# Moving the experts' weighing and the first batch's key squares from VectorE to ScalarE

## What is computed

```python
# layer 0, feed-forward: 8 experts, 128 wide, two per token
expert_w = jnp.einsum('tk,tke->te', top_k_weights, one_hot)
h1 = jnp.einsum('th,efh->tef', x, W1)
h3 = jnp.einsum('th,efh->tef', x, W3)
g = jax.nn.silu(h1) * h3 * expert_w[:, :, None]
out = jnp.einsum('tef,ehf->th', g, W2)

# layer 1, cross-attention: keys and queries normalised per head
def _rmsnorm(t):
    return t * jax.lax.rsqrt(jnp.mean(t * t, axis=-1, keepdims=True) + EPS)
```

## Time and profile before

| what | value |
|---|---|
| median of 3 runs (lowest to highest) | 1713.43 us (1712.78 to 1719.2) |
| profiled execution | 1715.07 us |
| its span in the trace | 1713.2 us |
| TensorE busy | 1599.9 us, 93% |
| VectorE busy | 1390.3 us, 81% |
| ScalarE busy | 1380.8 us, 81% |
| GpSimd busy | 1149.0 us, 67% |

### The profile page before, as it was taken

How to read it: one execution, slowest core, us unless ns; L and a number is a source line. 1 busy time by engine, 2 the same in 40 slices (tenths; PEclk the granted TensorE clock), 3 DMA queues, 4 the chain that set the end, 5 groups by cost and what they waited for, 6 DMA issues and landing times. The chain is left out here.

```text
span 1713.2 us, 43864 instructions
## 1 busy us (share of the span) xinstructions
PE 1599.9 (93%) x15829; PEld 1012.0 (59%) x16022; DVE 1390.3 (81%) x3487; ACT 1380.8 (81%) x2317; POOL 1149.0 (67%) x1770
## 2 busy tenths in 40 slices
PE   3799999999999899999999999988998999999997
PEld 1466777767767677767777777766563333333332
DVE  8889999999999989999989888889996755555422
ACT  4688888888888788878878888874337999999996
POOL 3558778787787877788888788865775655545200
PEclk9799999999999999999999999998999999999998
DMA  4299999999989999999989999997323232222100
GB/s 175 80 182 199 200 210 199 198 217 214 199 189 200 196 195 184 226 207 205 194 186 219 221 203 200 204 196 183 115 44 113 44 80 39 45 39 45 28 12 14
DMA packets 608872, 261.11 MB, mean 152 GB/s; under 512 B 576528, under 2 KB 581648, under 8 KB 607248
## 3 DMA queue, kind: packets, MB, share of 16 engines
q1 hardware_dynamic: 604432, 258.05, 70.4%
q10 hardware_dynamic: 4224, 0.25, 0.2%
HBM read 99.15 MB, written 17.29 MB: 68 GB/s over the span
## 5 line engine op out<-in xcount | busy, mean ns | idle before, releaser
L1754 PE MATMUL pv<-PT,VV 128*128 128x256 bf16 (+1 forms) x2880 | 341.5, 275 | 13.1 <-DMA PT<-PB 12.9
L1494 ACT ACTIVATE PB<-S,rsum 128x1024 bf16<-128x1024 f32 (+1 forms) x256 | 246.4, 988 | 105.9 <-DVE rsum L1260 81.0
L1754 PEld LDWEIGHTS pv<-PT,VV 128*128 128x128 bf16 (+1 forms) x2880 | 281.0, 99 | 81.6 <-issue 36.3
L1734 PE MATMUL score<-KK,QT 128*128 128x512 bf16 (+2 forms) x1795 | 314.6, 318 | 12.3 <-DVE mxp L1229 5.4
L1251 DVE SCALAR_TENSOR_TENSOR PB<-S,rsum,PB 128x1024 bf16<-128x1024 f32 (+1 forms) x256 | 295.8, 1156 | 2.7 <-ACT PB L1494 2.7
L1734 PEld LDWEIGHTS score<-KK,QT 128*128 128x128 bf16 x1920 | 158.2, 98 | 142.8 <-DVE mxp L1229 11.3
L1484 ACT ACTIVATE S<-S,nmx 128x1601 f32<-128x1601 f32 x128 | 210.2, 1642 | 7.3 <-DVE nmx L1241 7.2
L2621 ACT ACTIVATE P<-score 128x1024 f32<-128x1024 f32 x196 | 199.1, 1060 | 9.5 <-PE score L2713 5.9
L1072 POOL TENSOR_SCALAR S<-S,rsum 128x256 f32<-128x256 f32 x128 | 70.6, 551 | 130.5 <-DVE rsum L1260 116.4
L1613 PE MATMUL tb<-stage,wsb 128*128 128x512 bf16 x767 | 149.3, 337 | 5.8 <-DVE stage L631 3.9
L2733 PE MATMUL pv<-P,V 128*9 128x256 f32 (+1 forms) x2288 | 152.2, 380 | 1.3 <-ACT P L2621 0.8
(11 more groups left out here) (274 smaller groups left out, 3677.2 us busy)
## 6 DMA issues: line engine op xcount, KB each, us to landing
x<-rs_d SPq DMA_DIRECT2D x16, 936.0 KB, 5.1
rsb<-rs_d SPq DMA_DIRECT2D x16, 936.0 KB, 5.4
wsb<-w_split SPq DMA_DIRECT2D x46, 256.0 KB, 4.7
wsb<-w_split SPq DMA_DIRECT2D x23, 512.0 KB, 4.9
wpr<-in_wprojT SPq DMA_DIRECT2D x23, 512.0 KB, 6.6
context_d<-stage SPq DMA_DIRECT2D x16, 400.2 KB, 3.9
l_ctx<-context_d SPq DMA_DIRECT2D x4, 1601.0 KB, 7.4
rawh<-in_w_all SPq DMA_DIRECT2D x12, 512.0 KB, 5.7
```

Of the source, the lines that this page charges most:

```text
L1494: e.activation(m.PB[n % 2][:, 2 * a:a + b], m.S32[n % 2][:, a:b], ACT.Copy, scale=m.rsum[n % 2][:, 1:2]).then_inc(s["p_hi"], 1)
L1734: i = e.matmul(m.score[:, at:at + b - a], qt[:, kind, qp, q * P:(q + 1) * P], kk[:, kp, a:b], start=(k == 0), stop=(k == 2))
L1754: i = e.matmul(m.pv[:, at:at + 256], vv[0:rows, v, t, :], m.PT[k % 2][0:rows, turned(c, a), :], start=(c == first and r == 0), stop=(c == ...
```

## The change

Two pieces of VectorE's work go to ScalarE. The weighing of a half step, one VectorE instruction over 512 columns with a broadcast operand, becomes four ScalarE activations over 128 columns, each with one expert's weight as a per-partition factor (`act_weigh`). It is called behind `act_turn(n - 1)` in the loop, for step 0 behind the preparation of its chunk and for step 1 behind the cast of w2. The square of kn, for the first batch only, becomes an activation behind the value copy; VectorE's sum waits for it on `l1_sq`.

```diff
@@ attention of ScalarE, at it == NGB
             act_up(e, m, s, 0)
             for what, c in ffn_slots(0):
                 act_prepare(e, m, s, 0, what, c)
+            act_weigh(e, m, s, 0)
             act_up(e, m, s, 1)
             act_raw_high(e, m, s, 2)
+            act_weigh(e, m, s, 1)
@@
+def act_weigh(e, m, s, n):
+
+    t, hf, i = n // 2, n % 2, n % 2
+    e.wait_ge(s["f_act"], n + 1)
+    e.wait_ge(s["route_step"], ROUTER_STEPS * (1 if t < EARLY else 2))
+    if n >= 2:
+        e.wait_ge(s["f_turned"], n - 1)
+    for j in range(EH):
+        x = hf * EH + j
+        r = e.activation(m.f_g[i][:, j * FF:(j + 1) * FF], m.f_th[i][:, j * FF:(j + 1) * FF], ACT.Copy,
+                         scale=m.route["ew"][:, t, x:x + 1])
+    r.then_inc(s["f_gate"], 1)
@@ dve_up
     e.tensor_tensor(th[:, :], th[:, :], h3, ALU.mult).then_inc(s["f_act"], 1)
-    e.wait_ge(s["f_act"], n + 1)
-    if n >= 2:
-        e.wait_ge(s["f_turned"], n - 1)
-    w = m.route["ew"][:, t, hf * EH:(hf + 1) * EH].unsqueeze(2).broadcast_to([P, EH, FF])
-    e.tensor_tensor(m.f_g[i][:, :].rearrange("p (a b) -> p a b", a=EH),
-                    th[:, :].rearrange("p (a b) -> p a b", a=EH), w, ALU.mult).then_inc(s["f_gate"], 1)
@@ act_feed_forward
         if n <= 2 * NT:
             act_turn(e, m, s, n - 1)
+        if 2 <= n < 2 * NT:
+            act_weigh(e, m, s, n)
@@ dve_prepare, "product"
-        e.wait_ge(s["l1_kn"], k + 1)
-        e.tensor_tensor(m.l1_sq[0:rows, :], kn[0:rows, :], kn[0:rows, :], ALU.mult).then_inc(s["l1_sq"], 1)
+        if b:
+            e.wait_ge(s["l1_kn"], k + 1)
+            e.tensor_tensor(m.l1_sq[0:rows, :], kn[0:rows, :], kn[0:rows, :], ALU.mult).then_inc(s["l1_sq"], 1)
         e.wait_ge(s["l1_sq"], k + 1)
@@ act_prepare, "product", b == 0
+        k, rows = place(b, c), l1_rows(c)
         product_out(e, m, s, b, c)
+        e.wait_ge(s["l1_kn"], k + 1)
+        e.wait_ge(s["l1_ss"], k)
+        e.activation(m.l1_sq[0:rows, :], m.l1_kn[k % 3][0:rows, :], ACT.Square).then_inc(s["l1_sq"], 1)
```

## The result

The changed kernel took 1721.01 us in the median of 22 runs (1712.88 to 1724.43), the kernel before 1716.87 in the median of 22 (1710.04 to 1722.14). The ratio is 1.0024, with a 95% interval of 1.0012 to 1.0035: some 4.1 us slower, between 2.1 and 6.0. That is less than the 0.5% (8.6 us) up to which the prediction calls a time "same". The forecast was 1717.1 with a range up to 1720.6, so the time lies 0.4 above the range, while the step from before to after (+3.65 forecast) lies inside the measured interval. The base moved instead: the median of three runs was 1713.43, that of 22 runs 1716.87.

A forecast was written before the change was run, and what follows sets the result against it. The prediction took TensorE's 5.63 us step as the bound, VectorE only during the backlog of steps 8 to 11. Start 0.77, stage end 1.58 and clock 1.3 summed to 3.65 on 1713.43: 1717.1, range 1711.8 to 1720.6.

The forecast's parts named there:

- The loop over two engines: Feed-forward steps: VectorE's products, ScalarE's weigh, kn, V, square, then VectorE's sum and stacking form a loop of 5.46 us.
- The working through the steps: Steps 8 to 15, worked out instruction by instruction: the backlog remains and down(15) starts 1.58 us late without the clock.
- The prices on ScalarE: Per step, four weighing activations take 1.30 us, 1.20 until the next start; a square takes 0.40.
- The start: Stage start: square and weighing delay tanh(1) by 1.47 us, 0.45 returned by a faster GpSimd subtraction; everything to down(0) 0.77 late.
- The clock at the end: A 3.2 us TensorE wait ahead of down(14) lowers the granted clock, doubling down(14)'s 12 matmuls: 1.3 us.
- rival 4: Something outside the stage moves by over 0.5% either way; chance 0.05 slower, with the runs' scatter, 0.02 faster.
- Rival 1: Stage follows TensorE's pace alone and the kernel becomes faster, by 0.8 or 1.45 us, to 1712.0; chance 0.22.
- Rival 2: ScalarE's order costs 2.35 us but neither TensorE hole, at stage start or end, lowers the clock: 1715.8; chance 0.2.
- Rival 3: Both holes lower the clock: 5.35 us slower, 1718.8, or near 1720.5 with the upper ScalarE price; chance 0.16.

The follow-up runs named there:

- e1_weigh_only: The changed kernel with the squares back on VectorE, so only the weighing is on ScalarE; ratio to before 1.0017.
- e4_filled: The changed kernel with ten unused TensorE matmuls ahead of down(14); ratio to before 1.0001.
- e5_start: The changed kernel with weigh(0) moved ahead of the first chunk's kn and V on ScalarE; ratio to before 1.0013.
- e2: The changed kernel with the weighing back on VectorE, so only the squares are on ScalarE; ratio to before 0.9979.
- e7: The kernel before with only the two long tanh of steps 8 and 9 moved earlier on ScalarE; ratio to before 1.0011.
- e8: The changed kernel with the weighing back on VectorE and the two long tanh moved earlier on ScalarE; ratio to before 0.9989.
- e11: The kernel before once more, unedited; one run, 1715.72 us.
- e3: The changed kernel with the two long tanh of steps 8 and 9 moved earlier on ScalarE, ahead of the turn's copy; ratio to before 0.9990.
- e10: The changed kernel once more, unedited; ratio to before 1.0019.
- e6: The changed kernel with both the two long tanh earlier and weigh(0) ahead of the first kn; 1712.65 us beside 1715.47, ratio 0.9978.
- e9: e6 with six unused TensorE matmuls in each of three holes, ahead of down(0), down(14) and down(15); ratio to before 0.9989.

## Why the prediction was right or wrong

**The loop over two engines: right.** I had put it at 5.46, and the products stand 5.44 apart, at 1266.80 and 1272.24 and so on to 1288.56. One correction: e1_weigh_only shows that the loop is there without the square on ScalarE, through kn. The square is only one of its links.

**The working through the steps: right.** Against the start of up(8), in us, predicted and measured: down(8) 13.53 and 13.41, chunk(10) 15.83 and 15.79, up(11) 17.12 and 17.09, down(9) 20.24 and 20.19, up(12) 23.28 and 23.24, down(10) 26.23 and 26.11, up(13) 29.27 and 29.16, products(15) 45.52 and 45.42, down(14) 48.08 and 47.87. Down(15) with the clock was to be 51.41 + 1.3 = 52.71 and came at 52.71, but that it fits to the last digit is luck: without the fall it came at 51.20 (e4_filled, e5_start), 0.21 early, and the fall cost 0.21 more than I had put. So the delay without the clock is 1.37 and not 1.58. So an order could be worked out here to 0.2 over eight steps from the durations of one trace, if every instruction of the in-order queue is put in.

**The prices on ScalarE: right.** Four weighings took 1.26 to 1.28, and 1.18 to 1.20 to the next start, where the earlier trace rows gave 1.30 and 1.20. The square took 0.42, with 0.40 forecast. The Trainium skill, "ScalarE: Activation LUTs", section "What ACT_TABLE_LOAD costs", gives 186 ns and 0.833 ns an element, 93 ns more for a pointer operand and 93 ns of overlap, from which four come out at 1.26 us as an estimate (the prediction has 1.27); the trace agrees.

**The start: right in size, for a reason that was wrong.** 0.77 was forecast, 0.92 and 0.90 were measured (0.78 against the second trace of before). I gave 0.45 back because VectorE's square was to leave GpSimd alone. GpSimd's subtraction L1061 ahead of V(0), in the kernel before, after, with the squares alone moved and with the weighing alone moved, there with VectorE's square beside it:

```profile
1201.18 2.57 POOL L1061 TENSOR_TENSOR wpb<-rawh,wpb 128x1024 bf16<-128x1024 f32 x1
```

```profile
1197.98 2.13 POOL L1061 TENSOR_TENSOR wpb<-rawh,wpb 128x1024 bf16<-128x1024 f32 x1
```

```profile
1200.24 2.57 POOL L1061 TENSOR_TENSOR wpb<-rawh,wpb 128x1024 bf16<-128x1024 f32 x1
```

```profile
1201.77 2.12 POOL L1061 TENSOR_TENSOR wpb<-rawh,wpb 128x1024 bf16<-128x1024 f32 x1
1202.67 1.50 DVE L2413 TENSOR_TENSOR l_sq<-l_kn 128x256 f32<-128x256 f32 x1 [1.20 <-ACT l_kn L2599]
```

Without the square on VectorE it still takes 2.57, without the weighing 2.12. It was 2.57 in all five traces where VectorE weighs (before, e2, e7, e8, e11), and 2.12 to 2.13 in the eight where ScalarE does. So the weighing took the 0.45 from GpSimd, not the square; it was luck that both left VectorE in the same edit. The square was the one that suffered, 2.32 in the earlier trace rows and still 1.50 in e1_weigh_only: it began while L1061 ran and ended 0.28 or 0.29 behind L1061's end, in all four traces where the two meet (before, e1, e7, e11), whatever its own start. The weighing began 0.25 ahead of L1061 in the kernel before and took 0.84, where 0.69 is usual. The Trainium skill, "GPSIMD Engine Reference", section "Key points", says that GpSimd shares its SBUF interfaces with VectorE and contends with VectorE's instructions of two SBUF inputs. Both the weighing and the square are such, and these rows agree.

**The clock at the end: right in this kernel, but not as a rule.** A fall was forecast at 1.3. It cost 1.51 in the first trace (4.84 from down(14) to down(15) instead of 3.33) and 1.30 in the second (4.63). The reason I gave, a wait longer than one of 2.95 that had cost, doesn't hold. The waits of TensorE ahead of down(0) and down(14), with what followed:

| the clock behind it | waits (run) |
|---|---|
| fell | 2.34 (e2), 2.40 (e1), 2.89 (e7), 3.09 (e3, e10) ahead of down(0); 2.94 (after), 2.95 (e10) ahead of down(14) |
| stayed | 1.52 to 2.01 (e5, e6, before, e11), 2.30 (e8), 2.89 (after), 3.09 (e4) ahead of down(0); 2.45 (e1), 2.94 (e5) ahead of down(14) |

The same wait of 2.89, of 2.94 or of 3.09 did both, and what decides isn't shown by any run here. In these two places no wait of up to 2.01 was followed by a fall. In layer 1 it did fall, though the last waits ahead of it were 1.41, 0.90 and 0.61 at most, in traces with a fall (e6) and without one (e2) alike.

**What was left out: layer 1's first microseconds.** Their clock fell in seven traces (after, e3, e5, e6, e7, e8, e9) and not in six (before, e1, e2, e4, e10, e11), at 1.0 to 2.0 us a time. It fell and it stayed for the same kernel, after and e10_after_again, so it isn't shown to be the change's. The 1.2 of the first trace was in no term of my sum and in no rival.

**The step that failed: the base from which the numbers follow.** The forecast of 1717.1 is 3.9 under the measured 1721.01. Of this 3.4 is the base and 0.5 the change (4.1 instead of 3.65). I added 3.65 to 1713.43, the median of three runs, as if that were the kernel's level, and widened the range only for the mechanisms, with the runs' own scatter at the slow end of rival 4. Over 22 runs the kernel before is at 1716.87; beside the experiments its medians were 1716.77, 1715.47 and 1717.33. From 1716.87 the forecast would have been 1720.5, 0.5 from the measured 1721.01. The kernel scatters over 1710.0 to 1722.1. Medians of three drawn at random from its 22 runs lie between 1712.3 and 1721.2 in 95 of 100 draws, some 4 us either way, and that is as large as the whole effect. The row to see it by was at hand: of the three runs one was at 1719.2, 5.8 above the median, and the profiled execution was at 1715.07, 1.6 above it. The range should have had those 4 us beyond the mechanisms' ends: about 1708 to 1725.

A part of the scatter arises ahead of the stage, in code that no edit touches, and goes with the clock. In the 13 traces tanh(0) starts anywhere from 1194.30 to 1199.30. What the granted clock fell short of full, added up over windows of 8 us to 1192, is 18.6 to 20.6 us in the four traces that start it by 1195.4 (after, e4, e6, e10), and 22.2 to 23.8 in the six that start it at 1197.7 or later (before, e1, e5, e8, e9, e11). The three between them are mixed (20.4 in e2, 22.2 in e7, 23.9 in e3). In the timed runs too the time goes with the mean granted clock: it is 0.984 and 0.985 in the two fastest of the 22 runs of the kernel after (1712.88 and 1713.28) and 0.977 in the slowest (1724.43), with a correlation of -0.8 over all 22. That the two go together is shown; what makes the clock fall more in one execution than in another isn't.

**The rivals.** Rival 1, faster, fell by the loop, though its gain at the stage's late part is real once the tanh are out of the row (e3_tanh_early, e6_both) or the weighing stays (e2_square_only). Rival 2, no fall, is what e5_start did at the stage's end. Rival 3, both falls, is what e10_after_again did. The two traces of after are thus my forecast and my rival 3, of one and the same kernel.

## What to carry to other kernels

Moving work from a busy engine to an idle one was paid for here not by its duration but by where it stood in the second engine's order. If it waits for engine A and stands ahead of something that A waits for, the two become one loop; list that loop link by link, compare it with the pace of the bounding engine, and look for long unrelated work in the same row, since a loop only just under the pace can't work off a backlog. The mend that worked here is to put the unrelated work, and the moved work where it can, into a wait that is there anyway. And a forecast in absolute time is no better than its base: three runs don't give the level of a kernel that scatters by 12 us.

## What the runs showed of the hardware

- Under one and the same wait of TensorE (2.89, 2.94 or 3.09) the granted clock fell to 0.50 in one execution and not in another. A fall cost 1.3 to 1.7 us each time in the stage and 1.0 to 2.0 in layer 1. Single falls were read in the traces and not counted over the timed runs; but over the 22 runs of the kernel after the time goes with the mean granted clock (0.985 to 0.977, correlation -0.8).
- VectorE's weighing (two inputs in SBUF, one of them broadcast) beside GpSimd's subtraction made the latter 2.57 instead of 2.12 to 2.13, in every trace alike. VectorE's own square (two inputs in SBUF) that began while the subtraction ran took 1.50, 1.63, 2.32 or 2.34 instead of 0.42, and each time ended 0.28 or 0.29 behind the subtraction, which it didn't lengthen (2.12 in e1_weigh_only).
